# Conditioned transformer layer: row maxima of the first five batches turned in uneven groups of heads, first layer's output product inside the second attention

## The reference

```python
c6 = silu(c) @ Wc + bc
sh_msa, sc_msa, g_msa, sh_mlp, sc_mlp, g_mlp = split(c6, 6)
xm = ln(x) * (1 + sc_msa) + sh_msa
q, k, v = xm @ Wq + bq, xm @ Wk + bk, xm @ Wv + bv      # 16 heads of 16
w = softmax(q @ k.T / 16)
x = x + g_msa * ((w @ v) @ Wo + bo)
xm2 = ln(x) * (1 + sc_mlp) + sh_mlp
x = x + g_mlp * (gelu(xm2 @ W1 + b1) @ W2 + b2)
```

## Time and profile before

| | us |
|---|---|
| median of 3 runs (711.32 to 712.41) | 712.37 |
| profiled execution | 711.79 |
| its span | 710.0 |
| PE busy in it | 677.9 |
| DVE busy in it | 550.1 |
| ACT busy in it | 398.0 |

### The profile page before, as it was taken

How to read it: one execution, slowest core, us unless ns; L and a number is a source line. 1 busy time by engine, 2 the same in 40 slices (tenths; PEclk the granted TensorE clock), 3 DMA queues, 4 the chain that set the end, 5 groups by cost and what they waited for, 6 DMA issues and landing times.

```text
span 710.0 us, 15781 instructions
## 1 busy us (share of the span) xinstructions
PE 677.9 (95%) x6491; PEld 416.9 (59%) x6491; DVE 550.1 (77%) x1006; ACT 398.0 (56%) x474; POOL 237.1 (33%) x179
## 2 busy tenths in 40 slices
PE   7997899699999999999999999999999989999987
PEld 5542335354587447853687448853687437833976
DVE  4996898969877989689867988689867985762654
ACT  6532676168634884278634875278535871388231
POOL 1680003212263046312362046312452223250444
PEclk9997999999999999999999999999999998999999
DMA  8635002710262106330362115330351102011110
GB/s 312 196 108 157 18 17 78 209 61 32 87 186 63 61 32 175 82 107 31 95 177 65 59 38 173 79 120 17 112 160 41 68 32 63 31 62 63 47 37 30
DMA packets 58104, 63.57 MB, mean 90 GB/s; under 512 B 7560, under 2 KB 49054, under 8 KB 58030
## 3 DMA queue, kind: packets, MB, share of 16 engines
q1 hardware_dynamic: 58032, 62.56, 29.2%
HBM read 24.15 MB, written 12.89 MB: 52 GB/s over the span
## 4 chain that ended last, share of the span: by engine, by line
PE 80%; DVE 9%; issue 4%; ACT 3%; SPq 1%; POOL 1%; DMA 1%; ACTq 0%; DVEq 0%; POOLq 0%
PE ps L755 22%; PE ps L810 14%; PE ps L701 14%; PE ps L864 12%; DVE mx L1165 5%; PE ps L761 5%; PE ps L940 3%; PE ps L981 2%; PE ps L747 2%; PE ps L947 2%; ACT prob L642 1%; SPq L436 1%; PE ps L989 1%; PE ps L708 1%; ACT z L620 1%
## 5 line engine op out<-in xcount | busy, mean ns | idle before, releaser
L1165 DVE TENSOR_REDUCE mx<-ps 128x1 f32<-128x512 f32 x512 | 330.4, 685 | 54.1 <-PE ps L761 33.2
L642 ACT ACTIVATE prob<-ps 128x1024 f32<-128x1024 f32 x256 | 248.6, 1022 | 119.0 <-PE ps L755 57.5
L755 PE MATMUL ps<-qst,kst 98*32 98x512 bf16 x1920 | 144.1, 381 | 1.5 <-ACT prob L642 1.5
L810 PE MATMUL ps<-prob,vaug 128*32 128x512 f32 x1024 | 134.8, 597 | 0.7 <-DVE x L1340 0.4
L755 PE MATMUL ps<-kst,qst 96*32 96x512 bf16 x1336 | 129.9, 386 | 1.8 <-DVE mx L1165 0.9
L582 POOL TENSOR_TENSOR hl<-z,hh 128x512 fp32r<-128x512 f32 x64 | 82.2, 1286 | 123.0 <-DVE hh L1355 123.0
L688 ACT ACTIVATE z<-ps,bias_t 128x512 f32<-128x512 f32 x64 | 43.7, 686 | 119.5 <-PE ps L864 113.6
L755 PEld LDWEIGHTS ps<-qst,kst 98*32 98x32 bf16 x1920 | 53.4, 97 | 70.7 <-issue 27.4
L755 PEld LDWEIGHTS ps<-kst,qst 96*32 96x32 bf16 x1336 | 37.5, 95 | 73.6 <-DVE mx L1165 40.2
L701 PE MATMUL ps<-w_hi,hh 128*128 128x256 f32 x256 | 74.2, 290 | 2.5 <-POOL hl L582 2.5
L761 PE MATMUL ps<-kst,qst 96*128 96x512 bf16 x206 | 67.5, 389 | 7.2 <-DVE mx L1165 6.5
(11 more groups left out here) (120 smaller groups left out, 923.9 us busy)
## 6 DMA issues: line engine op xcount, KB each, us to landing
qst<-prob SPq DMA_DIRECT2D x96, 128.0 KB, 3.2
kst<-prob SPq DMA_DIRECT2D x96, 128.0 KB, 3.3
y_scratch<-rb SPq DMA_DIRECT2D x28, 256.0 KB, 2.0
xd<-in_x_dram SPq DMA_DIRECT2D x8, 512.0 KB, 3.8
xa<-in_x_dram SPq DMA_DIRECT2D x7, 512.0 KB, 4.7
yc<-y_scratch SPq DMA_DIRECT2D x14, 256.0 KB
rb<-r_scratch SPq DMA_DIRECT2D x14, 256.0 KB
out_dram<-xn SPq DMA_DIRECT2D x7, 512.0 KB, 3.2
```

The lines of the kernel that those rows point to most:

```text
L642: act.activation(prob[:, s % 2, 2 * p:2 * p + 2, :], ps[:, 2 * p:2 * p + 2, :], ACT.Exp, scale=1.0 / DH).then_inc(exp_done, 1)
L755: m = pe.matmul(out[32 * n:32 * n + 32, :], weights[:, 32 * n:32 * n + 32], moving, start=True, stop=True, skip_group_check=True)
L810: m = pe.matmul(ps[32 * q:32 * q + 32, 4 + g % 2, :], vaug[par][:, kt, G * g + q, :], prob[:, s % 2, q, :], start=kt == 0, stop=kt == TT - ...
L1165: dve.tensor_reduce(mx[:, t, h:h + 1], ps[:, banks[n], :], AXX, ALU.max).then_inc(max_done, 1)
```

## The change

The row maxima get a numbering over all batches (block q, 0 to 511), and `ROW_ENDS` says behind which heads a batch's maxima are turned: four groups for batch 0, groups ending at heads 8, 12 and 16 for batches 1 and 2, two halves for batches 3 and 4, one turn for the others. Where a group ends, PE's transposes stand directly behind its last block and DVE's two row instructions directly behind that block's reduction. The tables for the first five attentions and remainders (`C_FIRST`, `REST_FIRST`) give how many blocks of the old batch and of the new one each place takes: 25 blocks of batch 0 stand before its attention, 39 in it; of batches 1, 2, 3 and 4 there are 41, 49, 56 and 59 before theirs. Attentions wait for the load of a group's rows where its heads begin.

The product Wo of batch 0, the normalisation of y before it and the residual behind it move into the second attention's inner steps 1 and 2, with banks 5 and 7, while blocks have bank 6 alone until inner step 3; the second normalisation of batch 0 moves three inner steps later. The parts of batches 1 and 2 get homes in other buffers (`part_of`: xn2, xd, yc, xa, z), so that the first two attentions' exponentials wait for their own stack and for the last part, and the loads of xd and xa for the stack instead. SP's order in steps -1 and 0 changes with this, the reciprocal moves ahead by one q/k product in step 0, the memsets of vaug move ahead of the second half of the weights' split on POOL, and the idle products before the first two attentions go. Eleven blocks have a copy on PE that nobody reads, in place of 28.

```diff
+C_STEADY = ((0,) * STEPS, (1, 1) + (3,) * (STEPS - 4) + (4, 3))
+REST_STEADY = 0, (1, 1), 0, (0, 1, 0, 1), (0, 1, 0, 1), (1, 1, 1), (2, 2, 2, 2, 2, 0, 0, 0)
+C_FIRST = {
+    0: ((4,) * 9 + (3,) + (0,) * 6, (0,) * 9 + (1,) + (4,) * 6),
+    1: ((3, 2, 2, 2, 3, 3, 3, 3, 2) + (0,) * 7, (0,) * 8 + (1,) + (3,) * 7),
+    2: ((1, 1, 3, 3, 3, 3, 1) + (0,) * 9, (0,) * 6 + (2,) + (3,) * 9),
+    3: ((1, 1, 3, 3) + (0,) * 12, (0,) * 4 + (3,) * 11 + (4,)),
+    4: ((1, 1, 3) + (0,) * 13, (0,) * 3 + (3,) * 12 + (4,)),
+}
+REST_FIRST = {
+    -1: (2, (4, 0), 3, (0, 2, 0, 2), (1, 1, 1, 1), (), (8,)),
+    0: (0, (1, 1), 3, (0, 2, 0, 2), (1, 1, 1, 1), (), (3,)),
+    1: (0, (1, 1), 0, (0, 1, 0, 1), (0, 1, 0, 1), (2, 2, 2), (3, 3, 3, 2, 2, 2, 0, 0)),
+    2: (0, (1, 1), 0, (0, 0, 0, 0), (0, 0, 0, 0), (3, 3, 3), (3, 3, 3, 3, 2, 2, 0, 0)),
+    3: (0, (1, 1), 0, (0, 1, 0, 1), (0, 1, 0, 1), (2, 2, 2), (2, 2, 2, 2, 2, 0, 0, 0)),
+    4: (0, (1, 1), 0, (0, 1, 0, 1), (0, 1, 0, 1), (2, 2, 2), (3, 3, 2, 2, 2, 0, 0, 0)),
+}
+ROW_ENDS = {0: (4, 8, 12, 16), 1: (8, 12, 16), 2: (8, 12, 16), 3: (8, 16), 4: (8, 16)}
...
+TURN_BEHIND = {BLOCKS * b + group_blocks(b, g): (b, g) for b in ROW_ENDS for g in range(row_groups(b))}
...
+def score_banks():
+    taken, order, bank_of, before = {}, 0, {}, {}
+    def take(what, banks):
+        nonlocal order
+        bank = min(banks, key=lambda n: taken.get(n, (-1,))[0])
+        bank_of[what], before[what] = bank, taken[bank][1] if bank in taken else None
+        taken[bank] = order, what
+        order += 1
...
+                if i == 1 and s <= WO_FIRST + 1:
+                    blocks(n, (6,), (6,))
+                    continue
...
+        if i < 1:
+            blocks(ahead, (6, 7, 0, 1), (0, 1))
+        else:
+            blocks(ahead, (6, 7))
+        blocks(sum(up) + sum(down), (6, 7, 1) if 1 <= i <= 4 else (6, 7))
...
+WO_FIRST, WO_BANKS, WO_FIRST_BANKS = 2, (4, 5), (5, 7)
+BANK_OF, BEFORE = score_banks()
...
+IDLE_START, IDLE_ATTENTION = (10, 2, 3, 6), (0, 0)
...
+        def part_of(b, n, part):
+            if b not in PART_HOMES:
+                return parts[:, ORDER[n], part, :]
+            home, slot = divmod(3 * n + part, 4)
+            home = {"xa": xa, "xn2": xn[1], "xd": xd, "yc": yc, "z": z1}[PART_HOMES[b][home]]
+            return home[:].rearrange("p n f -> p (n f)").bitcast(BF16)[:, slot * S:(slot + 1) * S]
...
+                def load_maxima(b, g):
+                    first, last = group_heads(b, g)
+                    sp.wait_ge(mrow_done, 2 * rows_before(b, g) + 2)
                     for n in range(2):
-                        sp.dma_start(stack[MROW + n:MROW + n + 1, first:last, :], mrow[0:last - first, n, :]).then_inc(loaded, 16)
-                if runs(i, 0) and not later(i, 0, 1):
-                    sp.wait_ge(mrow_done, 2)
-                    load_maxima(qst[par], NH // 2, NH, m_loaded)
+                        sp.dma_start(qst[b % 2][MROW + n:MROW + n + 1, first:last, :], mrow[0:last - first, n, :]).then_inc(m_loaded, 16)
+                inner = range(1, row_groups(i)) if runs(i, 0) else ()
...
+                        if g + 1 in inner and i > 0:
+                            load_maxima(i, g + 1)
                         sp.wait_ge(y_evac, NG * i + g + 1)
                         sp.dma_start(y_scr[G * g:G * (g + 1)].rearrange("h r s -> (h r) s"), ysb[:, g % 2, :]).then_inc(y_written[g % 2], 16)
+                        if g + 2 in inner and i == 0:
+                            load_maxima(i, g + 2)
...
+                if i == -1:
                     fill_stack(1, 0)
                     fill_stack(1, 2)
+                    load_maxima(0, 0)
                     sp.wait_ge(low_split, 4)
                     sp.wait_ge(krows_set, 1)
                     sp.dma_start(kst[1][MROW:KROWS, :, :], kst[0][MROW:KROWS, :, :]).then_inc(krows_copied, 16)
                     fill_stack(1, 1)
-                    sp.wait_ge(half_rows, 2)
-                    load_maxima(qst[1 - par], 0, NH // 2, half_loaded)
+                    load_maxima(0, 1)
                     fill_stack(1, 3)
                 elif runs(i, 2):
-                    fill_stack(i + 2, 0)
-                    fill_stack(i + 2, 1)
+                    fill_stack(i + 2, 0, (0,) if i == 0 else (0, 1, 2))
+                    if i != 0:
+                        fill_stack(i + 2, 1)
                 if runs(i, 0) and not final(i):
                     sp.wait_ge(rec_done, i + 1)
                     sp.dma_start(r_scr.rearrange("h (a s) -> (h a) s", s=NH * S // P), rec).then_inc(r_written, 16)
-                if runs(i, 2) and not (early(i) and later(i, 2, 1)):
+                if runs(i, 2) and i > 0:
                     fill_stack(i + 2, 2, (0,))
+                elif i == 0:
+                    fill_stack(i + 2, 0, (1, 2))
...
+                    load_maxima(1, 0)
+                    fill_stack(i + 2, 1)
+                    fill_stack(i + 2, 2)
+                elif i == -2:
+                    fill_stack(i + 2, 2)
+                if runs(i, 2) and i != -1:
                     fill_stack(i + 2, 3)
                 if early(i) and not later(i, 2, 1):
                     modulation_rows()
-                if runs(i, 1) and not early(i):
-                    sp.wait_ge(mrow_done, 2 * i + 4)
-                    load_maxima(qst[1 - par], 0, NH, m_loaded)
+                if runs(i, 1) and i > 0:
+                    load_maxima(i + 1, 0)
...
+                    if i < 2:
+                        act.wait_ge(part_l, 4 * (i + 2))
                     for m in range(KC):
-                        act.wait_ge(stack_loaded[m], STACKED * (i + 2) if runs(i, 1) else STACKED * NB)
+                        act.wait_ge(stack_loaded[m], STACKED * (i + 1 if i < 2 else min(i + 2, NB)))
...
+            def taken_by(what):
+                if isinstance(what, tuple):
+                    pe.wait_ge(mrow_done, 2 * rows_before(*what) + 2)
+                elif what is not None:
+                    pe.wait_ge(max_done, what + 1)
             def scores(i, par, blocks, product=whole, copy=None):
-                banks, back = max_of(i + 1)
                 for _ in range(blocks if runs(i, 1) else 0):
-                    n = block_at[0]
-                    block_at[0] = (n + 1) % (NH * TT)
-                    h, t = n // TT, n % TT
-                    if back[n]:
-                        pe.wait_ge(max_done, 64 * (i + 1) + n - back[n] + 1)
+                    q = block_at[0]
+                    block_at[0] = q + 1
+                    h, t = q % BLOCKS // TT, q % TT
+                    taken_by(BEFORE[q])
                     if t == 0 and h % 8 == 0:
                         pe.wait_ge(stack_loaded[h // 8], STACKED * (i + 2))
-                    if n == 0:
-                        if later(i, 1, 1):
-                            pe.wait_ge(mrow_done, 2 * (i + 1))
-                    if banks[n] in (4, 5):
-                        spare_used[banks[n]] = 64 * (i + 1) + n + 1
-                    product(ps[:, banks[n], :], qst[1 - par][0:MROW, h, t * P:(t + 1) * P], kst[1 - par][0:MROW, h, :]).then_inc(s_done, 1)
+                    if BANK_OF[q] < 6:
+                        spare_used[BANK_OF[q]] = q + 1
+                    product(ps[:, BANK_OF[q], :], qst[1 - par][0:MROW, h, t * P:(t + 1) * P], kst[1 - par][0:MROW, h, :]).then_inc(s_done, 1)
                     if copy is not None:
                         whole(ps[:, copy, :], qst[1 - par][0:MROW, h, t * P:(t + 1) * P], kst[1 - par][0:MROW, h, :])
-            def turn_maxima(i, first=0, last=NH, turned=mt_done, bank=6):
-                if runs(i, 1):
-                    pe.wait_ge(max_done, 64 * (i + 1) + TT * last)
-                    if bank == 4:
-                        pe.wait_ge(vaug_done, 4)
-                    for t in range(TT):
-                        m = pe.transpose(ps[0:last - first, bank, t * P:(t + 1) * P], mx[:, t, first:last], ident[:])
-                    m.then_inc(turned, 1)
+                    if q in TURN_BEHIND:
+                        turn_maxima(*TURN_BEHIND[q])
+            def turn_maxima(b, g):
+                first, last = group_heads(b, g)
+                pe.wait_ge(max_done, BLOCKS * b + group_blocks(b, g))
+                taken_by(BEFORE[b, g])
+                for t in range(TT):
+                    m = pe.transpose(ps[0:last - first, BANK_OF[b, g], t * P:(t + 1) * P], mx[b % 2][:, t, first:last], ident[:])
+                m.then_inc(mt_done, 1)
...
+                    pe.wait_ge(m_loaded, 32 * rows_before(b, 1))
+                    spare_free(0)
+                    spare_free(1)
...
+                        for g in range(1, row_groups(i)):
+                            if s * G == group_heads(i, g)[0] * TT:
+                                pe.wait_ge(m_loaded, 32 * rows_before(i, g + 1))
+                        if i == 1 and s == WO_FIRST + 2:
+                            pe.wait_ge(x1_gated, 1)
...
```

(65 more changed lines are left out.)

334 lines of the change are left out of this document (147 added, 187 removed).

## The result

The changed kernel took 724.68 us (median of four executions: 720.38, 723.57, 725.80, 728.30) against 712.39 before; the ratio is 1.0166, 95% interval 1.0141 to 1.0191. It is slower, as forecast, and inside the range. The profiled execution took 720.38 us (span 718.6, mean granted clock 0.982).

The account below looks back on a forecast made before the run. PE was taken to decide from 147.4 us and not to be full before. Terms -11.2 + 3.1 - 0.6 + 2.5 + 13.8 = +7.6 on 711.79 gave 719.4, with 0.6 for the median 720.0 us; range 707 to 728.

Parts of the forecast that it names:

- start of the first attention: Up to the first attention's second step: fewer blocks and a smaller turn ahead, so it begins at 54.2 for 65.36, -11.2 us.
- first attention: Inside the first attention: two turns more at 2.75 us, +5.5, less 2.4 for a low clock saved, +3.1 us.
- its end to batch 1's first products: From the first attention's end to the second's first products: these start at 134.9 for 141.89 (old clock), -7.0 us.
- from there to step 4: Opening of the second attention: normalised y, one-bank blocks, a turn and Wo give back the 7 us won, +6.4 us.
- rest of the second attention: Second attention behind its fourth step: one more turn, 1.45, and two normalisations in the same steps, 1.0; +2.5 us.
- later stages: Remainders 1 to 4 and attentions 2 to 4: blocks left over at 0.215 us each and inner turns, +13.8 us.
- wait of 4.4 us at block 32: Before the transposes of batch 1's first group, amid the q/k products: PE waits 4.4 us that it did not before.
- The second rival: After the 4.4 us wait amid the q/k products the clock falls to 0.50: +3, 723 us; chance 0.07.
- The first rival: Opening of the second attention gained whole: fourth step 10.2 us earlier in place of 0.6, 710.4 us; chance 0.27.
- third rival: Dear turns: the eight in stages that PE fills cost 2.75 us each, 730 us, half of it 725; chance 0.10.
- the fourth's half of 1.45: Change comes out even: turns cost half of 1.45 us, saving 5.8, and the opening a little; 712 to 714; chance 0.11.
- The signs: Expected in the profile: first attention about 50 us, periods about 94, 83, 82, 82, idle PE ahead of inner turns.

## Why the prediction came out as it did

Its terms beside what the traces give, in us:

| term | forecast | measured |
|---|---|---|
| start of the first attention | -11.2 | -11.9 |
| first attention | +3.1 | -0.5 |
| its end to batch 1's first products | -7.0 | -8.0 |
| from there to step 4 | +6.4 | +12.2 |
| rest of the second attention | +2.5 | +4.0 |
| later stages | +13.8 | +12.8 |
| sum | +7.6 | +8.6 |

**Start of the first attention**: right, by its steps. The turn waits 1.19 for its last maximum in place of 2.2, the rows are used at 50.49, and step 1 begins at 53.47 with the clock at 1.00.

**First attention**: the step that failed is "the transposes stand directly behind the group's last block in PE's order", as the section on the change has it too. In the table of turns they stand one block later, since block 32, counted from 0, is the first behind a group of 32. DVE then has that block to reduce while PE transposes, as DVE's timeline of the changed kernel shows, which answers to the earlier trace rows:

```profile
54.77 2.58 DVE L1228 TENSOR_REDUCE mx<-ps 128x1 f32<-128x512 f32 x4 [0.39 <-PE ps L827]
57.54 0.68 DVE L1277 CAST mrow<-ps 4x512 bf16<-4x512 f32 x1 [0.19 <-PE ps L872]
58.25 0.68 DVE L1279 TENSOR_TENSOR mrow<-ps,mrow 4x512 bf16<-4x512 f32 x1
58.86 1.27 DVE L1228 TENSOR_REDUCE mx<-ps 128x1 f32<-128x512 f32 x2
```

From the last reduction's end, 57.35, to the next at 58.86 are 1.5 us, for 2.75 before. Three such turns for the one of before are +1.75, and with the clock's -2.4 that makes -0.65; measured -0.5. With the turns put where the prediction read them, the first attention (first products to its end) takes 50.66 in place of 49.13. So the place is 1.5 of the 3.6 us missed. The other 2.1 are the price: in that kernel, too, a turn holds the reductions for 2.0 us, not 2.75, as its DVE timeline shows between the end of the first row, 56.93, and the start of the second:

```profile
54.94 1.99 DVE L1228 TENSOR_REDUCE mx<-ps 128x1 f32<-128x512 f32 x3 [0.39 <-PE ps L827]
...
58.94 1.87 DVE L1228 TENSOR_REDUCE mx<-ps 128x1 f32<-128x512 f32 x3
```

The 2.75 of the kernel before contain 0.66 of waiting for the next product (at 85.22).

**To the first products**: right in size by wrong reasons. The wait of 4.4 us at block 32 did not come, for the same misreading. In its place came the row load, which the prediction lets land freely because "it moves ahead of three stack fills in SyncE's queue"; it overlooked the wait for the reciprocals' write in the same queue.

**From the first products to step 4**: the largest miss, 5.8 us. The chain was the right one (blocks in one bank, the normalised output on DVE, the products, the residual), priced at full clock, with 1.15 for a block in one bank that took 1.42. The second rival, the low clock, happened, for 15 us and more. That it would follow from a wait ahead of the opening was the wrong half: with the wait filled it came too. The pauses before 60 us that it takes to be about as long as 4.4 are short as well; in PE's row of the kernel before the longest is 1.49:

```profile
57.71 0.39 PE L761 MATMUL ps<-kst,qst 96*128 96x512 bf16 x1 [1.49 <-DVE mx L1165]
```

With the output ahead the low clock came as well, and the stretch was 9.4 us shorter all the same. What the runs show is that the output inside makes the opening long. Of the 9.4 the clock looks like a small part: between means of 0.64 and 0.81 the stretch differs by 1.4. How the rest divides between the single bank, DVE's 3.5 us for the normalised output and PE's waits in order was not taken apart further. The Trainium skill, on the page "TensorE: Matmul & The Clock Gate", section "A second HAM failure mode: psum-queue depth-cycling", tells of a kernel throttled by many short idles between groups of products as it cycles through PSUM banks; the trace agrees, with 0.50 for 10 us behind holes of at most 1.36 us in the run with the earlier row load.

**The first rival**, the opening gained whole, fell by this stretch: PE reached the first products 5 us earlier than forecast and lost it all by step 4.

**The rest of the second attention**, 1.5 us more than forecast: one turn (idle 1.30 at 160.28), the clock at 1.2 GHz for the first 0.8 us (a mean of 0.99 over the stretch), and the crowding by the two normalisations, in which one block at 174.63 waits 0.82. How the 4.0 divide between these was not tried.

**Later stages**: forecast +13.8, measured +12.8. The sizes were off in opposite ways: a block 0.30 for 0.215, a turn 1.5 in a remainder and 1.8 in an attention for 1.45, but three turns found their maxima ready (no idle worth the name ahead of those at 197.98, 344.56 and 397.02). Here is the answer to where the gain went: at step 4 the change is 8.2 us ahead only because 22 blocks are left over (50 done of batches 1 and 2, counted from the tables, against 72) and groups are still to be turned. Stages that PE fills take the blocks back at 22 x 0.3 = 6.6 us. That leaves 10.2 of the 16.8 for the eight inner turns that follow in place of three ordinary ones; at the prediction's 0.45 for an ordinary one an inner one comes to 1.44, close to its 1.45: an estimate, in which all else behind step 4 is counted to the turns. The run with the output ahead says the same: it stood 16 us ahead at step 4 (138.44) and ended even in the medians. With 1.54 and 1.80 measured for a turn, the third rival's 2.75 and the fourth's half of 1.45 are out.

**The signs** came out mixed. From the second inner step of one attention to that of the next it took 83.66, 82.05 and 81.67 us for batches 2, 3 and 4, as forecast, but 99.28 for batch 1 in place of 94; the first attention took 46.15 for 50, and the 4 us of idle PE ahead of batch 1's first group were 1.02. Turns without idle PE ahead, a sign of being wrong, were three of the eight.

**The median.** The prediction put it 0.6 above the profiled execution, and it is 4.3 above. The longer executions have the lower mean clock: 0.968 over 726.5 us is 46 us at 1.2 GHz (twice 0.032 of the span), 0.982 over 718.6 is 26. With the output ahead the clock was 0.986 to 0.993 in all twelve. Where the additional stretches at 1.2 GHz lie in the longer executions was not seen, since only one of each kernel is profiled. Behind the first products of batch 5, where all these kernels do the same, the profiled executions took from 247.8 us (one turn less) to 251.2 (output ahead).

## What to carry to other kernels

Work moved forward out of a starved stretch only pays if the stages that take it are not full: count what is left undone at the landmark where the gain is read, and price it there. An operation set amid a thin opening can cost far more than its own time, here 8 to 9 us for 3 us of products (136.81 to 139.85); that it is the banks and the DVE time which it takes from its neighbours is argued, not shown apart. And for each transfer that must be early, read what its queue waits for ahead of it, and for each wait the exact place in the order, by index.

## What was not expected of the hardware

A granted clock of 0.50 came without a long idle stretch: PE busy 2.68 of 5 us, with holes of 0.36 to 0.80 there and of 1.36 at most ahead, was followed by 10 us at 1.2 GHz. And a mean clock of 0.90 in place of 0.76 left the 16 us of the opening as they were (16.29 and 16.15): the time at the low clock and the time lost to it are not the same number.
